# The time loop of the first layer: both products of tanh in one VectorE operation of 256 columns, written to SBUF

## What is computed

```python
kn = k_t / (norm(k_t) + 1e-06)
retrieved = einsum('bnij,bnj->bni', S, kn)
delta = v_t - retrieved
outer = delta[..., :, None] * kn[..., None, :]
S_upd = tanh(beta_t[..., None] * S + outer)
S_new = (1.0 - w) * S + w * S_upd
Sq = einsum('bnij,bj->bni', S_new, q_t)
```

## Time and profile before

| | us |
|---|---|
| median of 3 runs | 8101.09 |
| lowest, highest run | 8098.16, 8102.05 |
| profiled execution: span from the first to the last instruction | 8086.1 |
| time loop of the first layer (from 157 to 2297 in the span) | 2140 |

### The profile page before, as it was taken

The page is one execution under the profiler, slowest core; times in us unless marked ns, Lnnn a source line. Parts: engine busy times, 40 slices in busy tenths (PEclk is TensorE's granted clock), DMA queues, the critical chain, the costliest instruction groups (busy, mean ns, idle before and its releaser), DMA issues. The chain is left out here.

```text
span 8086.1 us, 238265 instructions
## 1 busy us (share of the span) xinstructions
PE 6855.1 (85%) x89449; PEld 3959.4 (49%) x89449; DVE 6089.8 (75%) x13229; ACT 2874.3 (36%) x5767; POOL 3687.9 (46%) x4646
## 2 busy tenths in 40 slices
PE   4999999999977565787876899999999999999997
PEld 2666666666642222253343454545555545555553
DVE  7777777777775669696884777777777877777776
ACT  2111111111125132413213455554555554555554
POOL 0333333333310000030201777777777777777774
PEclk7999999999988776898987999999999999999999
DMA  0000000000000000000002222222222222222222
GB/s 21 1 0 0 0 0 0 0 1 0 1 6 1 0 15 0 0 1 0 1 1 93 83 67 74 72 70 71 73 70 74 71 75 73 73 71 72 71 70 72
DMA packets 213313, 292.27 MB, mean 36 GB/s; under 512 B 27872, under 2 KB 193280, under 8 KB 206592
## 3 DMA queue, kind: packets, MB, share of 16 engines
q1 hardware_dynamic: 212224, 277.76, 11.4%
HBM read 235.94 MB, written 13.66 MB: 31 GB/s over the span
## 5 line engine op out<-in xcount | busy, mean ns | idle before, releaser
L2915 POOL TENSOR_TENSOR big<-big 128x512 f32<-128x512 f32 x776 | 1076.6, 1414 | 62.5 <-DMA big<-norms 51.2
L834 POOL TENSOR_TENSOR big<-big 128x128 f32<-128x128 f32 x1024 | 415.3, 406 | 1339.9 <-DVE big L780 1339.5
L600 ACT ACTIVATE banks<-banks 128x128 f32<-128x128 f32 x1024 | 268.3, 262 | 1823.8 <-DVE banks L763 1823.8
L2270 PE MATMUL banks<-hidden,big 128*128 128x256 f32 x3104 | 791.8, 399 | 117.9 <-DVE big L2739 47.7
L1954 POOL TENSOR_TENSOR big<-big 128x448 f32<-128x448 f32 (+10 forms) x160 | 142.5, 891 | 1625.9 <-DVE weights_odd L1818 1553.9
L2332 PE MATMUL banks<-big,hidden 128*32 128x512 f32 x6144 | 793.2, 612 | 0.0
L489 PE MATMUL banks<-big 128*128 128x256 f32 x2050 | 732.6, 440 | 61.7 <-ACT big L574 59.4
L2311 PE MATMUL banks<-big 32*32 32x64 f32 (+1 forms) x49152 | 600.5, 225 | 193.6 <-issue 193.5
L2270 PEld LDWEIGHTS banks<-hidden,big 128*128 128x128 f32 x3104 | 575.5, 194 | 379.2 <-DVE big L2739 137.2
L2311 PEld LDWEIGHTS banks<-big 32*32 32x32 f32 x49152 | 519.1, 104 | 433.7 <-issue 433.4
L334 PE MATMUL banks<-big,weights_even 128*128 128x512 f32 (+5 forms) x1056 | 504.1, 670 | 248.5 <-DVE big L1086 45.1
(11 more groups left out here) (361 smaller groups left out, 14422.7 us busy)
## 6 DMA issues: line engine op xcount, KB each, us to landing
big<-norms SPq DMA_DIRECT2D x776, 128.0 KB, 2.9
big<-qk SPq DMA_DIRECT2D x50, 512.0 KB, 4.5
big<-vo SPq DMA_DIRECT2D x25, 1024.0 KB, 5.7
small<-tables SPq DMA_DIRECT2D x196, 128.0 KB, 2.3
weights_odd<-ffn SPq DMA_DIRECT2D x25, 537.5 KB, 5.7
big<-tables SPq DMA_DIRECT2D x98, 128.0 KB, 2.2
weights_even<-tables SPq DMA_DIRECT2D x98, 128.0 KB, 2.9
hidden<-big SPq DMA_DIRECT2D x171, 64.0 KB, 2.4
```

The source lines that it names most:

```text
L834: nc.gpsimd.tensor_tensor(full(u["kS"][s % 2]), full(S), by(u["ko_c"]), ALU.mult).then_inc(*e.did(("kS", s)))
L2270: mm = self.nc.tensor.matmul(bank[:, n * QTOK:(n + 1) * QTOK], u["w" + name.lower()][:, (2 * g + n) * P:(2 * g + n + 1) * P], u["xs"][:, a ...
L2915: self.nc.gpsimd.tensor_tensor(x, x, u["norms"][:, n, g].unsqueeze(1).broadcast_to([P, 2, QTOK]), ALU.mult).then_inc(*e.did(("scaled", f, ...
```

## The change

Three things change: the layout of b[7], the place of wT, and the two products of T, which become one operation of 256 columns. Its first input is T, taken twice; its second is the pair of coefficient columns (kw_c and w_c, now neighbours, as both_c); its output is the pair of kT and wT, side by side in SBUF (kwT). The waits for kT (TensorE, line 508) and for wT (VectorE, line 780) both name this operation.

```diff
-        S=[cut(0, 128), cut(128, 128)], aS=cut(256, 128), bS=cut(384, 128), kT=cut(512, 128),
-        kS=[cut(640, 128), cut(768, 128)], qd_c=cut(896, BATCH * STEPS), vb=[cut(1152, 256), cut(1408, 256)],
-        kn_c=by_step(2048), w_c=by_step(2304), om_c=by_step(2560), knext_c=by_step(2816), kw_c=by_step(3072),
-        ko_c=by_step(3328),
-        step_bank=core.bank[0:2], outer=core.bank[2][:, 0:128], wT=core.bank[2][:, 128:256],
+        S=[cut(0, 128), cut(128, 128)], aS=cut(256, 128), bS=cut(384, 128), kwT=cut(512, 256), kT=cut(512, 128), wT=cut(640, 128),
+        kS=[cut(768, 128), cut(1664, 128)], qd_c=cut(896, BATCH * STEPS), vb=[cut(1152, 256), cut(1408, 256)],
+        kn_c=by_step(2048), om_c=by_step(2304), knext_c=by_step(2560), ko_c=by_step(2816),
+        kw_c=by_step(3072), w_c=by_step(3328), both_c=cut(3072, 2 * BLK * STEPS).rearrange("p (k n s) -> p k n s", k=2, n=BLK),
+        step_bank=core.bank[0:2], outer=core.bank[2][:, 0:128],
@@
             dve.wait_ge(*e.after("T", s))
-            tt(cut(u["kT"]), cut(u["T"]), spread(u["kw_c"], s), ALU.mult).then_inc(*e.did(("kT", s)))
-            tt(cut(u["wT"]), cut(u["T"]), spread(u["w_c"], s), ALU.mult).then_inc(*e.did(("wT", s)))
+            tt(u["kwT"].rearrange("p (k n i) -> p k n i", k=2, n=BLK),
+               cut(u["T"]).unsqueeze(1).broadcast_to([P, 2, BLK, NST]),
+               u["both_c"][:, :, :, s].unsqueeze(3).broadcast_to([P, 2, BLK, NST]), ALU.mult).then_inc(*e.did(("kT", s)))
+            e.name_last("wT", s)
             dve.wait_ge(*e.after("aS", s))
```

## The result

The changed kernel takes 8020.87 us (median of 4 runs, 8013.89 to 8023.40) against 8099.62 (4 runs of the kernel before beside it): a ratio of 0.9905, 95% interval 0.9892 to 0.9919, so 66 to 87 us less. The forecast was 8045, 55 us less, with a range of 8020 to 8068.

A forecast was written before the change was run, and what follows sets the result against it. The time loop was taken as bound by each step's dependent chain, VectorE, ScalarE, VectorE. Span 8086.1 less 55.5 (sixteen turns of 3.5) gives 8030.6; plus 15.0 to the median, 8045 us, range 8020 to 8068.

The forecast's parts named there:

- The step: Time loop: from one product of T to the next, 1.96 us in place of 2.02.
- the slack of 0.19: Delta's path through line 508: usable at 0.87 us, outer product starts at 1.06; the change spends this slack.
- The gain per step: Steady step of the time loop: outer product starts at 1.00 in place of 1.06, so 0.06 us.
- wT in SBUF at nothing: S reading SBUF alone: bounds 0 and 0.01 us per step, taken as 0.
- The turns: Loop turns: about 3 steps gain nothing, start 0.13 later; 3.5 us gain per turn, 55.5 over sixteen.
- The base: Outside the span: median of the runs 15.0 us over the profiled span, left as it is.
- rival 1: Outer product: delta not last, VectorE's own chain bounds; gain 0.075 to 0.087 per step, 8024 us; chance 0.12.
- Rivals 2 and 3: Wide operation: 440 to 475 ns, 8065 to 8100 us (0.12); or not streaming, up to 580 ns, 8203 us (0.07).
- Rival 4: S with two SBUF inputs contends with GpSimd: up to 0.41 us per step, 420 us in all; chance 0.02.
- Rival 5: TensorE idles longer ahead of line 508, its clock falls: rounds of 2.57 us, 0.55 more per step; chance 0.03.

The follow-up runs named there:

- the swapped order: Kernel before with wT's product placed ahead of kT's, nothing else changed: 8090.2 us, step 2.029 us.
- the later delta: A second copy of line 525's bf16 product ahead of line 508, added to each kernel: before 8245.7 us, changed 8286.6 us.
- the second pair: Both kernels unchanged, run and profiled again: medians 8082.56 us (before) and 8022.71 us (changed), ratio 0.9925.

## Why the prediction was right or wrong, point by point

- *The step.* Forecast 1.96; measured 1.963 and 1.967. The wide operation was put at 420 ns and took 423; S follows its end by 0.035; the outer product starts at 0.458 + 0.325 + 0.221 = 1.004 (forecast 1.00). The forecast mechanism, the slack of 0.19 that the change spends to below zero, stands: the swapped order and the removal of line 508 gave the steps that it says, and so did the later delta in both kernels once its cost was taken as the measured 0.125. The rule of the gain can be read off: VectorE's own chain became 0.073 shorter (S at 0.458 in place of 0.531), but the delta came 0.133 later (423 in place of 290 ns), and of the slack of 0.191 only 0.058 was left to gain.
- *The gain per step.* 0.06 was forecast, 0.054 and 0.050 came. What was missed is the outer product itself: in the changed kernel, where it comes behind the delta, it takes 298 to 300 ns in place of 293, and arg starts 0.006 to 0.008 later behind it. The swapped kernel, where it waits for the delta too, has 299 ns as well, and the one without line 508 has 292.
- *wT in SBUF at nothing.* Alone it is worth 0.008 per step, at the writer's end. The bound of 281 ns for S, taken from line 734, was not reached.
- *The turns.* I charged 0.13 per turn and no gain in three steps. The steps 0 to 2 of a turn cost 17.4 us over the median step in the loop before and 13.5 in the changed one (first profiles), 16.0 and 15.8 in the second: no loss. The sum had no term for a change in the time at the lower clock, and that time moves between executions of one kernel: 83.7 and 79.6 us in the two loops of before, 63.0 and 72.8 in those of the changed kernel. How much of the 3.9 less in the first pair is the change and how much chance is open.
- *The stalls inside a turn.* Not in the sum at all, since I looked only at those of the turn itself. They fell by 7.0 us (7.2 in the second pair). The loop's 64.8 of the first pair is thus 55.2 from the step (0.054 x 1023), 7.0 from the stalls, 3.9 from the steps 0 to 2, less 1.3 in all other steps; 55.5 was forecast.
- *The base.* The term that was furthest off is this one: "The median of the runs is 15.0 over that span, which I leave". What lies around the span is 1.8 us (the changed kernel's profiled execution: 8023.4 with a span of 8021.6). The profiled execution of before thus took about 8087.9 and lay 13 us under the median; I carried that over to the changed kernel as if it were fixed, but its profiled execution lies 2.5 over its median, and in the second set that of before lies 11 over the median of 7. So it is no fixed part but moves from one execution to the next. 8045.6 less 9.3 (loop) less 13.2 (base) is 8023.1, against 8023.4 for the profiled execution.
- *The number.* The measured 8020.87 lies 0.9 above the lower end of the range, which was put there for rival 1. That it fell inside is in part luck. The mechanism came with the forecast step; of the 24 us below the forecast some 9 are the loop (the stalls and the steps at the turns), the others the scatter of the base.
- *Rivals.* The time fell on rival 1's (8024), but not by its mechanism: the delta is last. Rivals 2 and 3 are out by the 423 ns. Rival 4 is out here, as S meets no GpSimd operation, and is right one operation further on, as the outer product in SBUF shows. Rival 5 did not come (0.98 in the loop), but the kernel without line 508 shows how near it is: 0.85.

Whether the gain is 60 or 79 us by the runs stays open: the two intervals overlap from 66 to 74, and the two pairs of profiles give 64.5 and 68.0 in the span (some 8 of the 68.0 lie behind the loop, where nothing was changed). The changed kernel repeats (8020.9 and 8022.7); it is the kernel before that moved, from 8099.6 to 8082.6, and its later runs lie between 8072.3 and 8093.8.

## What to carry to other kernels

Joining two operations of a dependent chain takes away a start gap (0.21) and makes the first result come later (by 0.13): count the slack of everybody who waits for the part that used to come first, and expect the gain to end where that slack does. Read slack from start to start, not from the list of waits, which shows nothing while neighbouring operations overlap. And take the time around a span from a run that gives both, not from a median of other executions.

## What was not expected of the hardware

- A VectorE product of 128 columns takes 8 ns less into SBUF than into PSUM (281 and 289 ns; the outer product 291 and 299).
- An operation with a value per partition, 32 columns wide, takes 251 ns, and the next of its like starts 0.158 to 0.168 behind; four such in place of two of 128 made the step 0.20 us longer here.
- Two SBUF inputs beside GpSimd's product cost 0.13 us (299 to 427 ns), and nothing when GpSimd is idle (291 ns for S, as with one).
- In the three kernels with 64 more or fewer TensorE products in the body of the loop, the layers that come later were 130 to 195 us slower; why is open.
- With line 508 gone, TensorE's granted clock in the loop fell from 0.98 to 0.85, and the loop was 21 us longer though its median step was 0.021 shorter.
